# Head attention: the weights of two key chunks are added on GpSimd before TensorE sums them, and the ring of weights grows from two chunks to three

## The chip, the cores and the metric

The kernel runs on one core of a Trainium2 chip. A core has TensorE (PE, matrix products, with its own loads of weights, PEld), VectorE (DVE), ScalarE (ACT), GpSimd (POOL) and SyncE (SP, which here only issues transfers), and each works through its own list of instructions in order; between engines, semaphores say what may start. The metric is the device time of one execution in microseconds (us). Before the change it was 945.48 us, the median of three runs (945.34 to 948.28).

## The reference

Four layers follow each other on x of 8 x 256 x 512, each added to x: a latent cross-attention, a gated feed-forward layer, an eight-head attention against the context, and a layer of eight experts. The change touches the third only:

```python
def _L1_xattn_ref(q, k, v, gamma):        # q: layer norm of x; k = v = context
    qh = q.reshape(B, h, dq, Lq)           # h = 8 heads of 32 channels, Lq = Lk = 512
    qk = jnp.einsum('bhdq,bhdl->bhql', qh, kh) * scale
    sm = jax.nn.softmax(qk, axis=-1)
    ret = jnp.einsum('bhql,bhdl->bhdq', sm, vh)
    return gamma * ret.reshape(B, Dv, Lq)
```

A softmax needs, beside the weights exp(score - maximum), their sum over all 512 keys. That sum is what the change computes in another way.

## The kernel before

In `head_attention` (L721 and after) the channels lie on the partitions: a *unit* is one tile of 128 partitions, which is four heads (HU = 4) of 32 channels, and there are 16 units (NU). The 512 keys of a unit are four *chunks* of 128 (TC = 4). For each chunk c and each head h TensorE makes a tile of scores, 128 keys by 512 queries, in one of two PSUM buffers `B` (`scores`, L866), and ScalarE turns it into weights with an exponential into an SBUF tile `l_pt` (`weights`, L922). Then TensorE takes the four weight tiles of a chunk twice: as the moving operand of the product with the values (`product`, L877, into `PV`) and of a product with ones (`row_sums`, L885, into `SM`), which adds them over the keys. Both are f32 with a weight block of 32 columns, one for each head, so that the four heads lie side by side in the array. Both accumulate over the four chunks.

The weight tiles lie in a ring of RING = 2 chunks. ScalarE may overwrite a chunk when its row sums have been taken:

```python
wait(act, sum_ps, TC * u + c - RING + 1)
```

TensorE's order is written out by hand, as eight *cycles* (i = 0 to 7) a unit. Each has two score tiles, then in an even cycle a product and in an odd cycle the row sums of the same chunk, which lies one chunk back; odd cycles end with a quad of coarse scores (`a_quad`, L847) for a unit ahead, from which VectorE takes maxima (`maxima`, L983):

```python
scores(u, 2 * i)
scores(u, 2 * i + 1)
of, c = (u, i // 2 - 1) if i >= 2 else (u - 1, TC - 1)
if of >= 0:
    (row_sums if i % 2 else product)(of, c)
```

So in cycle 2 stands the product of chunk 0, in cycle 3 its row sums, in cycle 4 the product of chunk 1, in cycle 5 its row sums, and after these in cycle 5 the turn of the maxima (`rows`, L857). The quad in cycle 1 is that of (u + 1, 2), in cycle 3 of (u + 1, 3), in cycles 5 and 7 of (u + 2, 0) and (u + 2, 1).

VectorE's order in a unit: maxima (u + 1, 2), `statistics(u + 3)` (L988 to L992), maxima (u + 1, 3), `queries(u + 3)` (L997), maxima (u + 2, 0), `reciprocals(u - 1)` (L1001), maxima (u + 2, 1), `normalise(u - 1)` (L1007). ScalarE has beside the exponentials `result` after cycle 1 (L927), `totals` after 2 (L932), `logarithm` after 3 (L937) and `first_reciprocals` after 4 (L941), all of unit u - 1. GpSimd's order: `add(u - 2)` (L1076), `power(u + 3)` (L1050, waits for the statistics of VectorE), `keys(u + 3)` (L1057, L1059), `check_reciprocals(u - 1)` (L1072, waits for the reciprocals of ScalarE), `queries(u + 3)` (L1064, L1066). SyncE places the parts of keys and queries in `stack` (L809) a unit ahead.

Of the kernel before, what the change touches and what calls it, by code (L numbers as in the profile page):

```python
# [17 lines left out]
def wait(eng, sem, value):  # L18

    if isinstance(value, int) and value <= 0:  # L20
        return
    eng.wait_ge(sem, value)
# [700 lines left out]
def head_attention(nc, X, ident_f, ones_f, neg_half, ctx_in, ctxt_in, gamma_in, D, DH):  # L723
# [5 lines left out]
    CYCLES = STEPS // 2  # L729
    SCALE = float(DH) ** -0.5  # L730
    M0 = 3 * DH
    RING = 2
    st = ExitStack()
    with st:
        def sb(name, shape, dt=F32):
# [5 lines left out]
        def sem(name):  # L741
            return st.enter_context(nc.semaphore("l1_" + name))
# [24 lines left out]
        a_ps, max_ok, b_ps, b_ok = (sem(n) for n in ("aps", "max", "bps", "bok"))  # L767
        pv_ps, sum_ps, pv_ok, sums_ok = (sem(n) for n in ("pvps", "sumps", "pv", "sums"))
        ln_ok, r0_ok, sr_ok, ng_ok = (sem(n) for n in ("ln", "r0", "sr", "ng"))
        recip_ok, tx_ok, res_ok = (sem(n) for n in ("rec", "tx", "res"))  # L770

        block = st.enter_context(nc.Block())

# [15 lines left out]
        def weights_at(u, c, h):  # L789
            return PT[(TC * u + c) % RING][h]  # L790

# [45 lines left out]
        def _(pe):  # L837
# [40 lines left out]
                mm.then_inc(pv_ps, 1)  # L878

            def row_sums(u, c):  # L880
                if c == 0:
                    wait(pe, sums_ok, u)
                for h in range(HU):
                    cols = slice(DH * h, DH * h + DH)
                    mm = pe.matmul(SM[cols, :], ones_f[:, 0:DH], weights_at(u, c, h)[:, :], start=c == 0, stop=c == TC - 1)  # L885
                mm.then_inc(sum_ps, 1)

            for j in range(TC):
# [21 lines left out]
        @block.scalar  # L910
        def _(act):
            def rows_out(u):
                t = turn_of_rows(u)
                act.wait_ge(b_ps, t + 1)
                wait(act, row_in[u % 2], 16 * (u // 2))
                act.activation(mrow[u % 2][:, :], B[t % 2][0:HU * TC, 0:P], ACT.Copy).then_inc(b_ok, 1)

            def weights(u, s):
                c, h, t = s // HU, s % HU, turn_of_scores(u, s)
                act.wait_ge(b_ps, t + 1)  # L920
                wait(act, sum_ps, TC * u + c - RING + 1)
                act.activation(weights_at(u, c, h)[:, :], B[t % 2][:, :], ACT.Exp, scale=SCALE).then_inc(b_ok, 1)  # L922

            def result(u):
                act.wait_ge(pv_ps, TC * u + TC)
                wait(act, res_ok, u - 1)
                act.activation(pvs[u % 2][:, :], PV[:, :], ACT.Copy).then_inc(pv_ok, 1)  # L927

            def totals(u):
                act.wait_ge(sum_ps, TC * u + TC)  # L930
                wait(act, sr_ok, u)
                act.activation(sums[:, :], SM[:, :], ACT.Copy).then_inc(sums_ok, 1)  # L932

            def logarithm(u):
                act.wait_ge(sums_ok, u + 1)
                wait(act, recip_ok, u)
                act.activation(r0[:, :], sums[:, :], ACT.Ln).then_inc(ln_ok, 1)  # L937

            def first_reciprocals(u):
                act.wait_ge(ln_ok, u + 1)  # L940
                act.activation(r0[:, :], r0[:, :], ACT.Exp, scale=-1.0).then_inc(r0_ok, 1)  # L941

            def keys(u):
                act.wait_ge(kf_ok, 16 * u + 16)
                act.activation(kh[u % 2][:, :], kf[:, :], ACT.Copy).then_inc(kh_ok, 1)

            def queries(u):
                act.wait_ge(qf_ok, u + 1)
                act.activation(qh[u % 2][:, :], qf[:, :], ACT.Copy).then_inc(qh_ok, 1)

            act.preload_act_table_set("natural_log_exp_and_others")
            for u in range(2):
                keys(u)
                queries(u)
            rows_out(0)
            for u in range(NU):
                for i in range(CYCLES):
                    weights(u, 2 * i)
                    weights(u, 2 * i + 1)
                    if i == ROWS_AT // 2 - 1 and u + 1 < NU:  # L960
                        rows_out(u + 1)
                    if u:
                        if i == 1:
                            result(u - 1)
                        if i == 2:
                            totals(u - 1)
                        if i == 3:
                            logarithm(u - 1)
                        if i == 4:
                            first_reciprocals(u - 1)  # L970
            result(NU - 1)
            totals(NU - 1)
            logarithm(NU - 1)
            first_reciprocals(NU - 1)
# [71 lines left out]
        def _(pool):  # L1046
# [27 lines left out]
            def add(u):  # L1074
                pool.wait_ge(tx_ok, u + 1)
                pool.tensor_tensor(X[:, u, :], X[:, u, :], pvs[u % 2][:, :], ALU.add).then_inc(res_ok, 1)  # L1076

            for u in range(2):
                power(u)
                keys(u)  # L1080
                queries(u)
# [3 lines left out]
            for u in range(NU):  # L1085
                if u >= 2:
                    add(u - 2)
                if u + 3 < NU:
                    power(u + 3)
                    keys(u + 3)  # L1090
                if u:
                    check_reciprocals(u - 1)
                if u + 3 < NU:
                    queries(u + 3)
            add(NU - 2)
            check_reciprocals(NU - 1)
# [606 lines left out]
```

## Time and profile before

| | before |
|---|---|
| median of 3 runs | 945.48 us (945.34 to 948.28) |
| the profiled execution, its own time | 950.93 us |
| its span in the profile | 949.1 us |
| TensorE busy | 738.4 us (78%) |
| VectorE busy | 571.9 us (60%) |
| ScalarE busy | 400.9 us (42%) |
| GpSimd busy | 330.3 us (35%) |

The span is the stretch from the first to the last instruction of one profiled execution. Times of places are us from its start. "Busy" is the share in which an engine computes; the idle time that a row names is that just before its instructions, with what ended it. The profiled execution took some 5 us more than the median, so differences are worked out inside it and put on the median.

### The profile page before, as it was taken

How to read it: one execution, taken by the hardware profiler on the slowest of the kernel's cores; microseconds unless marked ns; L12 is line 12 of the kernel's file. 1: busy time of each engine (PE TensorE's matmuls, PEld its weight loads, DVE VectorE, ACT ScalarE, POOL GpSimd, SP SyncE). 2: the span in 40 equal slices, each digit the busy share in tenths (PEclk: the TensorE clock that was granted, in tenths of full speed). 3: DMA queues.
4: the chain of work that ended last, by engine and by line, in shares of the span. 5: the costliest groups of instructions: out<-in, count | busy, mean ns of one | idle time of the engine just before them, and what ended most of it. 6: DMA issues, size and time to landing. Idle time of an engine off the chain costs nothing. (4 is left out here: it accounts for less than half of the span.)

```text
span 949.1 us, 13635 instructions
## 1 busy us (share of the span) xinstructions
PE 738.4 (78%) x4259; PEld 308.5 (33%) x4288; DVE 571.9 (60%) x981; ACT 400.9 (42%) x727; POOL 330.3 (35%) x332
## 2 busy tenths in 40 slices
PE   3888888399999995699999999958002999999500
PEld 1344333144444442122222222135001555555300
DVE  5677775557668583889998898276300344344245
ACT  1534442164646462277877877845001222222100
POOL 2546454101120103235355443256471122122275
PEclk9999998779999998599999999979556999999955
DMA  7490100103030367343333332100355355655287
GB/s 265 77 122 24 44 1 0 62 0 108 15 122 2 121 250 271 83 105 98 96 96 96 96 101 73 30 1 1 119 205 145 100 124 134 134 129 130 79 261 256
DMA packets 98543, 99.12 MB, mean 104 GB/s; under 512 B 49448, under 2 KB 72872, under 8 KB 98224
## 3 DMA queue, kind: packets, MB, share of 16 engines
q1 hardware_dynamic: 90432, 78.25, 28.9%
q0 software_dynamic: 7328, 19.93, 8.7%
q8 instruction: 35, 0.57, 0.3%
q14 instruction: 28, 0.23, 0.1%
q10 hardware_dynamic: 720, 0.13, 0.1%
HBM read 51.82 MB, written 33.03 MB: 89 GB/s over the span
## 5 line engine op out<-in xcount | busy, mean ns | idle before, releaser
L983 DVE TENSOR_REDUCE l_negm<-l_a 128x2 f32<-128x1024 f32 x128 | 150.3, 1218 | 22.3 <-PE l_a L847 22.0
L922 ACT ACTIVATE l_pt<-l_b 128x512 f32<-128x512 f32 x256 | 138.9, 595 | 47.2 <-PE l_b L866 47.1
L1470 PE MATMUL ex_hp<-w1h,ex_xt 128*128 x312 | 78.6, 321 | 53.7 <-DMA ex_xt<-slots_x 53.4
L1556 POOL TENSOR_TENSOR ex_hl<-ex_hf,ex_hh 128x352 bf16<-128x352 f32 x39 | 33.2, 852 | 141.3 <-ACT ex_hh L1512 141.3
L866 PE MATMUL l_b<-l_stack 97*128 97x512 bf16 x256 | 79.4, 391 | 0.5 <-ACT l_pt L922 0.3
L568 PE MATMUL f_gp<-f_xt,wg 128*128 128x512 fp8e4 x256 | 67.4, 387 | 3.8 <-ACT f_y L611 2.7
L1490 PE MATMUL ex_yp<-w2h,ex_ht 128*128 (+1 forms) x215 | 68.8, 379 | 2.0 <-DVE ex_ht L1534 2.0
L877 PE MATMUL l_pv<-l_pt,l_vt 128*32 128x512 f32 x512 | 69.1, 612 | 0.0
L885 PE MATMUL l_sm<-l_pt,ones_f 128*32 128x512 f32 x512 | 68.3, 605 | 0.0
L1509 ACT ACTIVATE ex_hf<-ex_pre 128x352 f32<-128x352 f32 x39 | 19.3, 496 | 115.3 <-DVE ex_pre L1529 115.3
L568 PE MATMUL f_up_ps<-f_xt,wg 128*128 128x512 fp8e4 x256 | 67.0, 385 | 0.0
L1539 DVE COPY ex_y<-ex_yp 128x512 f32<-128x512 f32 x39 | 27.0, 691 | 53.3 <-PE ex_yp L1490 53.3
L717 POOL TENSOR_TENSOR X<-X,f_y 128x512 f32<-128x512 f32 x16 | 18.7, 1168 | 115.2 <-ACT f_y L611 115.2
L579 PE MATMUL f_yp<-wl,f_h 128*128 128x512 fp8e4 x256 | 55.9, 379 | 0.0
L1470 PEld LDWEIGHTS ex_hp<-w1h,ex_xt 128*128 128x128 bf16 x312 | 31.3, 100 | 69.3 <-issue 54.1
L670 DVE TENSOR_TENSOR f_prod<-f_gate,f_up 128x512 bf16<-128x512 bf16 x64 | 27.0, 422 | 43.9 <-ACT f_up L604 39.9
L1529 DVE TENSOR_TENSOR ex_pre<-ex_hp,ex_b1s 128x352 f32<-128x352 f32 x39 | 20.4, 524 | 54.0 <-PE ex_hp L1470 42.5
L1470 PE MATMUL ex_hp<-w1l,ex_xt 128*128 x156 | 50.2, 322 | 0.0
L602 ACT ACTIVATE f_gate<-f_gp 128x512 bf16<-128x512 f32 x64 | 38.2, 597 | 21.7 <-PE f_gp L568 21.7
L604 ACT ACTIVATE f_up<-f_up_ps 128x512 bf16<-128x512 f32 x64 | 38.2, 597 | 18.0 <-PE f_up_ps L568 18.0
L1490 PE MATMUL ex_yp<-w2l,ex_ht 128*128 (+1 forms) x117 | 44.3, 379 | 1.2 <-issue 0.2
L847 PE MATMUL l_a<-l_parts 32*128 32x512 bf16 x256 | 29.3, 408 | 17.5 <-DVE l_negm L983 10.5
(220 smaller groups left out, 1396.6 us busy)
## 6 DMA issues: line engine op xcount, KB each, us to landing
l_stack<-l_parts SPq DMA_DIRECT2D x192, 64.0 KB, 2.1
slots_x<-f_zeros SPq DMA_DIRECT2D x1, 9984.0 KB, 29.3
slots_y<-ex_y SPq DMA_DIRECT2D x39, 256.0 KB, 2.3
f_stage<-in_w SPq DMA_DIRECT2D x8, 704.0 KB, 4.0
l_ctx<-in_ctx SPq DMA_DIRECT2D x8, 512.0 KB, 5.3
f_stage<-in_w SPq DMA_DIRECT2D x8, 512.0 KB
l_kf<-in_ctx SPq DMA_DIRECT2D x16, 256.0 KB, 2.8
l_vt<-in_ctx_t SPq DMA_DIRECT2D x16, 256.0 KB, 3.0
```

What stands on the lines that cost most here:

```text
L568: mm = pe.matmul(bank[m % 2][:, :], wg8[:, c, col:col + P], xt8[:, c, :], start=c == 0, stop=c == FC - 1)
L579: mm = pe.matmul(YP[r % 2][:, :], h8[:, m, r * P:(r + 1) * P], wl8[:, m, :], start=m == 0, stop=m == HC - 1)
L602: act.activation(gate[m % 2][:, :], GP[m % 2][:, :], ACT.Gelu_apprx_tanh).then_inc(gate_ok, 1)
L604: act.activation(up[m % 2][:, :], UP[m % 2][:, :], ACT.Copy).then_inc(up_ok, 1)
L866: pe.matmul(B[t % 2][:, :], stack[u % 2][0:M0 + 1, 0, h, c * P:(c + 1) * P], stack[u % 2][0:M0 + 1, 1, h, :], start=True, stop=True).then_ ...
L877: mm = pe.matmul(PV[cols, :], VT[u % 2][:, c, cols], weights_at(u, c, h)[:, :], start=c == 0, stop=c == TC - 1)
L885: mm = pe.matmul(SM[cols, :], ones_f[:, 0:DH], weights_at(u, c, h)[:, :], start=c == 0, stop=c == TC - 1)
L922: act.activation(weights_at(u, c, h)[:, :], B[t % 2][:, :], ACT.Exp, scale=SCALE).then_inc(b_ok, 1)
L983: dve.tensor_reduce(negm[u % 2][:, 2 * half:2 * half + 2, j], A[half][:, :, :], AX.X, ALU.max, negate=True)\
L1470: mm = pe.matmul(HP[i % 2][:, 0:H], xt[i % AHEAD][:, xp * FC + f, :], w1p[wp][:, bass.ds(e, 1), f * H:(f + 1) * H], start=k == 0, stop=k = ...
L1490: mm = pe.matmul(YP[i % 2][:, :], ht[i % 2][0:K, n, m, :], w2p[wp][0:K, bass.ds(e, 1), m * D:(m + 1) * D], start=k == 0, stop=k == 3 * HC - 1)
L1556: pool.tensor_tensor(hl[i % 2][:, 0:H], hf[i % 2][:, :], hh[i % 2][:, 0:H], ALU.subtract).then_inc(hl_ok, 1)
```

## The change

GpSimd gets a new step, `pair_sums(u, h)`: for each of the four heads it adds the weights of chunk 1 to those of chunk 0, in the place of chunk 0, once the product of chunk 0 has read them and the weights of chunk 1 are there. TensorE leaves out the row sums of chunk 0 and takes those of the pair where those of chunk 1 stood, each head behind a wait of its own. The ring has three chunks, and the waits on `sum_ps` count three row sums a unit. In GpSimd's list three pair sums stand between `power` and `check_reciprocals`, the fourth behind it, and `keys(u + 3)` moves behind them.

```diff
-    RING = 2
+    RING = 3
+    SUMMED = (1, 1, 2, 3)
             def row_sums(u, c):
+
                 if c == 0:
+                    return
+                if c == 1:
                     wait(pe, sums_ok, u)
                 for h in range(HU):
                     cols = slice(DH * h, DH * h + DH)
-                    mm = pe.matmul(SM[cols, :], ones_f[:, 0:DH], weights_at(u, c, h)[:, :], start=c == 0, stop=c == TC - 1)
+                    if c == 1:
+                        pe.wait_ge(pair_ok, HU * u + h + 1)
+                    mm = pe.matmul(SM[cols, :], ones_f[:, 0:DH], weights_at(u, c if c > 1 else 0, h)[:, :], start=c == 1, stop=c == TC - 1)
                 mm.then_inc(sum_ps, 1)
@@ weights @@
-                wait(act, sum_ps, TC * u + c - RING + 1)
+                g = TC * u + c - RING
+                if g >= 0:
+                    act.wait_ge(sum_ps, (TC - 1) * (g // TC) + SUMMED[g % TC])
@@ totals @@
-                act.wait_ge(sum_ps, TC * u + TC)
+                act.wait_ge(sum_ps, (TC - 1) * (u + 1))
@@ gpsimd @@
+            def pair_sums(u, h):
+
+                pool.wait_ge(pv_ps, TC * u + 1)
+                pool.wait_ge(b_ok, done_scores(u, HU + h))
+                first, second = weights_at(u, 0, h), weights_at(u, 1, h)
+                pool.tensor_tensor(first[:, :], first[:, :], second[:, :], ALU.add).then_inc(pair_ok, 1)
+
@@ gpsimd, the loop over units @@
                 if u + 3 < NU:
                     power(u + 3)
-                    keys(u + 3)
+                for h in range(HU - 1):
+                    pair_sums(u, h)
                 if u:
                     check_reciprocals(u - 1)
+                pair_sums(u, HU - 1)
                 if u + 3 < NU:
+                    keys(u + 3)
                     queries(u + 3)
```

GpSimd's list of one unit before, from one `add` of `X` to the next `power`; l_rstd is written by `power`, l_parts by `keys` and `queries`, l_sr by `check_reciprocals`:

```order
L1076 TENSOR_TENSOR X<-X,l_pvs 128x512
L1050 TENSOR_TENSOR l_rstd<-l_veps,neg_half 128x1
L1057 CAST l_parts<-l_kf 128x512
L1059 TENSOR_TENSOR l_parts<-l_kf,l_parts 128x512
L1072 TENSOR_TENSOR l_sr<-l_sums,l_r 128x512
L1064 CAST l_parts<-l_qf 128x512
L1066 TENSOR_TENSOR l_parts<-l_qf,l_parts 128x512
```

And the same stretch now; L1091 is the new pair sum, and the other lines are some eight to ten further down in the file:

```order
L1084 TENSOR_TENSOR X<-X,l_pvs 128x512
L1058 TENSOR_TENSOR l_rstd<-l_veps,neg_half 128x1
L1091 TENSOR_TENSOR l_pt<-l_pt 128x512 x3
L1080 TENSOR_TENSOR l_sr<-l_sums,l_r 128x512
L1091 TENSOR_TENSOR l_pt<-l_pt 128x512
L1065 CAST l_parts<-l_kf 128x512
L1067 TENSOR_TENSOR l_parts<-l_kf,l_parts 128x512
L1072 CAST l_parts<-l_qf 128x512
L1074 TENSOR_TENSOR l_parts<-l_qf,l_parts 128x512
```

Three of the four pair sums stand behind `power` and ahead of `check_reciprocals`, the fourth behind both; the work on keys has moved behind all of them.

TensorE's list before, from the product of chunk 0 in cycle 2 to the turn of the maxima in cycle 5, with the semaphores that each waits for:

```order
L877 MATMUL l_pv<-l_pt,l_vt 32x512 x3
L866 MATMUL l_b<-l_stack 128x512 [waits l1_bok] x2
L885 MATMUL l_sm<-l_pt,ones_f 32x512 [waits l1_sums]
L885 MATMUL l_sm<-l_pt,ones_f 32x512 x3
L847 MATMUL l_a<-l_parts 128x512 [waits l1_max]
L847 MATMUL l_a<-l_parts 128x512
L847 MATMUL l_a<-l_parts 128x512 [waits l1_max]
L847 MATMUL l_a<-l_parts 128x512
L866 MATMUL l_b<-l_stack 128x512 [waits l1_bok] x2
L877 MATMUL l_pv<-l_pt,l_vt 32x512 [waits l1_bok]
L877 MATMUL l_pv<-l_pt,l_vt 32x512 x3
L866 MATMUL l_b<-l_stack 128x512 [waits l1_bok] x2
```

And now, from the scores of cycle 3 to the quad of cycle 5:

```order
L867 MATMUL l_b<-l_stack 128x512 [waits l1_bok] x2
L848 MATMUL l_a<-l_parts 128x512 [waits l1_max]
L848 MATMUL l_a<-l_parts 128x512
L848 MATMUL l_a<-l_parts 128x512 [waits l1_max]
L848 MATMUL l_a<-l_parts 128x512
L867 MATMUL l_b<-l_stack 128x512 [waits l1_bok] x2
L878 MATMUL l_pv<-l_pt,l_vt 32x512 [waits l1_bok]
L878 MATMUL l_pv<-l_pt,l_vt 32x512 x3
L867 MATMUL l_b<-l_stack 128x512 [waits l1_bok] x2
L891 MATMUL l_sm<-l_pt,ones_f 32x512 [waits l1_pair,l1_sums]
L891 MATMUL l_sm<-l_pt,ones_f 32x512 [waits l1_pair] x3
L858 MATMUL l_b<-ident_f,l_negm 16x128 [waits l1_bok,l1_max]
```

The row sums of cycle 3 are gone, and each of the four in cycle 5 waits for its own pair sum, `l1_pair`.

## Rows read from the trace of the kernel before

**Rows 1.** Busy time by stretch: units 1 to 12, units 13 and 14, unit 15.

```profile
409.12:574.80 165.68, 165.49 (x1180) 34.87 (x1177) 148.64 (x167) 130.21 (x252) 81.55 (x84) 1.00 0.38 97
574.80:601.91 27.11, 27.07 (x192) 5.58 (x189) 20.38 (x20) 21.70 (x42) 6.55 (x6) 1.00 0.32 79
601.91:616.30 14.39, 14.26 (x100) 2.71 (x96) 1.44 (x2) 11.17 (x22) 2.55 (x2) 1.00 0.01 1
```

The columns are the stretch, its length, then busy us and instructions of PE, PEld, DVE, ACT and POOL, the granted clock of TensorE, the share of the DMA engines, and GB/s.

**Rows 2.** Instructions in order of time, unit 12, TensorE: start, duration, instructions.

```profile
561.02 0.60 PE L866 MATMUL l_b<-l_stack 97*128 97x512 bf16 x2
561.56 1.07 PE L877 MATMUL l_pv<-l_pt,l_vt 128*32 128x512 f32 x8
...
563.09 1.06 PE L885 MATMUL l_sm<-l_pt,ones_f 128*32 128x512 f32 x8
564.09 0.40 PE L847 MATMUL l_a<-l_parts 32*128 32x512 bf16 x4
564.42 0.61 PE L866 MATMUL l_b<-l_stack 97*128 97x512 bf16 x2
564.96 1.07 PE L877 MATMUL l_pv<-l_pt,l_vt 128*32 128x512 f32 x8
...
569.88 1.06 PE L885 MATMUL l_sm<-l_pt,ones_f 128*32 128x512 f32 x8
570.77 0.38 PE L857 MATMUL l_b<-ident_f,l_negm 128*16 128x128 f32 x2
...
571.41 0.61 PE L866 MATMUL l_b<-l_stack 97*128 97x512 bf16 x2
...
574.80 0.60 PE L866 MATMUL l_b<-l_stack 97*128 97x512 bf16 x2
```

**Rows 3.** The same view and unit, the other engines.

```profile
564.52 2.36 DVE L983 TENSOR_REDUCE l_negm<-l_a 128x2 f32<-128x1024 f32 x2 [0.38 <-PE l_a L847]
...
566.79 0.68 DVE L988 BATCH_NORM_STATS2 l_st<-X 128x6 f32<-128x512 f32 x1
...
568.06 0.55 POOL L1050 TENSOR_TENSOR l_rstd<-l_veps,neg_half 128x1 f32<-128x1 f32 x1 [2.57 <-DVE l_veps L992]
...
569.21 0.63 ACT L941 ACTIVATE l_r<-l_r 128x512 f32<-128x512 f32 x1
```

**Rows 4.** Who waited for whom, from 395 to 617 us: total, times, longest.

```profile
POOL l_rstd L1050 <- DVE l_veps L992: 34.6, 13, 5.9
```

**Rows 5.** In order of time: two GpSimd sums of weight tiles in the first layer.

```profile
28.47 1.27 POOL L436 TENSOR_TENSOR l_psa<-l_pt 128x512 f32<-128x512 f32 x1 [5.61 <-ACT l_pt L289]
29.69 1.26 POOL L437 TENSOR_TENSOR l_psb<-l_pt 128x512 f32<-128x512 f32 x1
```

**Rows 6.** In order of time: VectorE and GpSimd at once, in two units.

```profile
422.69 1.07 DVE L1001 SCALAR_TENSOR_TENSOR l_sr<-l_sr,l_r 128x512 f32<-128x512 f32 x1 [0.67 <-POOL l_sr L1072]
423.30 1.49 POOL L1066 TENSOR_TENSOR l_parts<-l_qf,l_parts 128x512 bf16<-128x512 f32 x1
...
435.65 1.16 POOL L1066 TENSOR_TENSOR l_parts<-l_qf,l_parts 128x512 bf16<-128x512 f32 x1
```

**Rows 7.** In order of time: unit 0, GpSimd's power and TensorE's row sums of chunk 1.

```profile
400.52 0.55 POOL L1050 TENSOR_TENSOR l_rstd<-l_veps,neg_half 128x1 f32<-128x1 f32 x1 [2.13 <-DVE l_veps L992]
...
404.20 1.07 PE L885 MATMUL l_sm<-l_pt,ones_f 128*32 128x512 f32 x8
```

**Rows 8.** In order of time: TensorE in the first layer, two rounds of its loop.

```profile
47.91 0.38 PE L191 MATMUL l_sm<-l_dev,mean_f 128*128 128x1 f32 x2 [1.76 <-DVE l_dev L363]
48.15 5.38 PE L197 MATMUL l_pv<-l_pt,l_gx 128*128 128x512 f32 x8
...
68.17 0.38 PE L191 MATMUL l_sm<-l_dev,mean_f 128*128 128x1 f32 x2 [1.17 <-DVE l_dev L363]
68.42 3.68 PE L197 MATMUL l_pv<-l_pt,l_gx 128*128 128x512 f32 x8
```

**Rows 9.** Busy time by stretch, columns as in rows 1: inside the first of these rounds.

```profile
50.00:52.00 2.00, 2.00 (x3) 0.66 (x2) 0.72 (x3) 0.00 (x0) 1.53 (x2) 0.50 1.00 109
```

More of the change, by code:

```diff
@@ L769, in head_attention @@
         ln_ok, r0_ok, sr_ok, ng_ok = (sem(n) for n in ("ln", "r0", "sr", "ng"))
-        recip_ok, tx_ok, res_ok = (sem(n) for n in ("rec", "tx", "res"))
+        recip_ok, tx_ok, res_ok, pair_ok = (sem(n) for n in ("rec", "tx", "res", "pair"))
         block = st.enter_context(nc.Block())
```

## The prediction

> **What bounds the kernel now.** I read the busy time by stretch first, for the attention alone, since only it is changed. The reader is to see that TensorE has no idle time there: 165.49 us busy of 165.68 in units 1 to 12, which is 165.68 / 12 = 13.81 us a unit, at the full granted clock, with GpSimd busy for 81.55 us, 6.8 us a unit [rows 1]. So TensorE is the bound, GpSimd is half empty, and four f32 matmuls a unit less look like a gain. Whether they are one is told by the instructions in order of time, for one unit, since each engine works in order: what has to be seen is when, in a unit, GpSimd can begin, and when TensorE will want its result.
>
> All places below are counted from the first scores of a unit, 561.02 us for unit 12 [rows 2]. TensorE's times: quad (u + 1, 2) at +3.07, scores of cycle 2 at +3.40, product of chunk 0 at +3.94 for 1.07, so done at +5.0; row sums of chunk 1 at +8.86, the turn of the maxima at +9.75, the scores of cycle 6 at +10.39, and the next unit at +13.78 (574.80) [rows 2]. A pair of scores with a product is 561.56 - 561.02 = 0.54 and 1.00 more, about 1.53 us a cycle, and the quad another 0.33 (564.42 - 564.09) [rows 2].
>
> **What is saved.** The row sums of chunk 0 occupy TensorE for as long as those of any chunk do: from 563.09 to the quad at 564.09, 1.00 us [rows 2]. 16 units make 16.0 us, if what comes after in the unit can move up by as much. Nothing else of TensorE's goes.
>
> **What is added, and where it stands.** GpSimd gets 64 sums of 128 x 512 f32. The same form on weight tiles is in the first layer, 1.27 us each, and back to back they start 29.69 - 28.47 = 1.22 us apart [rows 5]. That is 4.9 us a unit: 6.8 + 4.9 = 11.7 of 13.8, so GpSimd's busy time would still fit. Its order does not.
>
> 1. The pair sums stand behind `power(u + 3)` in GpSimd's list. `power` waits for statistics which VectorE makes after the maxima of quad (u + 1, 2): the quad is at +3.07, VectorE starts on it at +3.50 (564.52) after an idle 0.38, the statistics start at +5.77 (566.79), and GpSimd's power runs from +7.04 (568.06) for 0.55 to +7.59 [rows 3]. That this is a real wait and no accident of one unit: GpSimd waited 34.6 us for it in 13 units [rows 4]. Nothing of the change moves it, as everything ahead of it in the unit stays where it was. So the first pair sum starts at about +7.56, 2.5 us after its operands are there.
> 2. Behind it: three pair sums, `check_reciprocals`, the fourth pair sum. The reciprocals that the check wants end at 569.21 + 0.63, +8.8 [rows 3], before the check's turn at 7.56 + 3 x 1.22 = +11.2, so nothing more is waited for. The fourth pair sum starts at 7.56 + 4 x 1.22 = +12.44 and ends 1.27 later, at +13.7. With 0.1 us for the semaphore (an estimate: VectorE starts at 564.52 on a quad that ends at 564.09 + 0.40 [rows 2, 3], 0.03 us, and I round up) TensorE's fourth row sum starts at +13.8.
> 3. TensorE wants it at +8.86 before, and, with the row sums of chunk 0 gone, about 1 us earlier. It stands at the head of TensorE's list in cycle 5, and behind it wait the turn of the maxima, the quad (u + 2, 0), and all scores of cycles 6 and 7; ScalarE has nothing to do without these. The heads before come at +8.9, +10.2 and +11.4, and are hidden.
> 4. One head alone needs two f32 passes one after another, as the four heads side by side do, so I take the same 0.89 us from its start to the turn of the maxima (569.88 to 570.77) and 1.53 to the scores of cycle 6 (571.41); from there the unit ends 3.39 later (574.80) as before [rows 2]. The new unit is 13.8 + 1.53 + 3.39 = 18.7 us, 4.9 more than 13.81. The 1.00 us saved lies inside the stall and buys nothing.
> 5. VectorE's `queries` now falls among the pair sums (it comes after maxima that end at about +9.4). Where the two engines met in the trace, GpSimd's 1.16 us became 1.49, 0.33 more, the first being that of 435.65, the second that of 423.30, behind VectorE's instruction of 422.69 [rows 6]. I add 0.3: 5.2 us a unit. From below this cost is 0 (VectorE may lose the race each time). The Trainium skill (SBUF — State Buffer, "Who interferes with whom") says that the pair of ports is an exclusive lock, held for the whole instruction by whoever starts first. By that rule the loser waits up to the 1.07 us which VectorE's instruction is shown with [rows 6], part of which was its own wait; charged in full it would be 12 x 0.7 = 9 us on the kernel above my sum, but the row shows 0.33, and I go by it.
>
> Units 1 to 12: 12 x 5.2 = 62.4 us.
>
> Unit 0 has no check, and its power runs from 400.52 to 401.07 [rows 7]. Four pair sums end at 401.04 + 3 x 1.22 + 1.27 = 405.97, with semaphore 406.1, where the row sums of chunk 1 started at 404.20 [rows 7]: 1.9 later, with the meeting of point 5 2.2 us.
>
> Units 13 to 15 have no power, so that the pair sums start when the product of chunk 0 is done, +5.1. Three of them end at +8.8, just as the reciprocals do [rows 3]; check and fourth sum follow to 8.8 + 1.22 + 1.27 = +11.3, TensorE starts at +11.4 where it was +8.86: 2.5 us each. Unit 14 and 15 have fewer quads, which shortens both sides alike to within 0.3 us: unit 15 was 8 x 1.53 = 12.3 and becomes 11.0 + 1.0 + 3.06 = 15.1. Together 7.7 us.
>
> The moved `keys(u + 3)` and `queries(u + 3)` (3.6 us of GpSimd) start at +13.7 and end at +17.4 of a unit of 19; what needs them is a unit ahead, and the next power is at +7.04 of the next unit, so the length of the unit hides them. SyncE's load of keys stands behind them at about +15.6; its next transfer, the stack of the next unit, waits for that unit's start at +19 anyway. VectorE's sequence from the quad of cycle 5 to its next maxima keeps its length, relative to the scores of cycle 6, so it still arrives in time. The third chunk of the ring gives ScalarE nothing: its exponentials follow scores, and TensorE's list sets these.
>
> **The sum.** 2.2 + 62.4 + 7.7 = 72.3 us on the profiled execution of 950.93, to 1023; on the median of 945.48, from which that execution is 5 us away for reasons that have no part in this, 1017.8. The forecast is 1018 us. Its own range is 1005 to 1032: 0.3 us a unit less for point 5 (4 us), 0.5 a unit either way for the gaps and the length of a lone head (8 us), 6 us more for the lock.
>
> **The rivals.**
>
> *TensorE's clock falls in the stall.* In the first layer TensorE was idle for 1.76 us before a short matmul [rows 8], and a little later its granted clock was 0.50, which is 1.2 GHz, while it was busy without a gap [rows 9]; the eight matmuls then took 5.38 us where they take 3.68 in another round [rows 8]: 1.7 us for one fall. In the new kernel TensorE has from about +8 to +13.8 only three lone heads of some 0.9 us, and before the fourth an idle 1.5 us, in every unit. For it speaks this likeness; against it, that the other round had 1.17 us idle at the same place and its eight matmuls ran at full pace [rows 8]. At 1.7 us in 15 units it adds 26 us, to 1044; if every unit pays the passes of the lone head and both last cycles in full at 1.2 GHz, 0.9 + 3.4 = 4.3 us, it is up to 64 more. Chance 0.26.
>
> *Power is no bar.* If VectorE's statistics came much earlier, the pair sums would start at +5.1 in all units, and the last at +10.1, as in units 13 to 15. The cost would be 15 x 2.5 + 2.2 = 40 us: 986. For it speaks that VectorE has idle time in a longer unit; against it, that the quad which it waits for is fixed at +3.07, and that GpSimd waited for power in 13 units [rows 4]. Chance 0.06.
>
> *The sums are hidden: faster.* If the fourth pair sum ended before TensorE comes to it at about +7.9, the row sums saved would all count: 16 x 1.0 = 16 us, 930. It turns at one place, the end of the fourth pair sum in cycle 5; from the product's end at +5.0 there are 2.9 us for 4.9 us of sums, even without power and check. For it speaks only GpSimd's idle half [rows 1]. Chance 0.02.
>
> *Something else by which the time stays near.* No mechanism that I can find; 0.01 within 0.3%, 0.01 a little slower.
>
> **How the numbers follow.** The forecast has 0.64. The range that is to hold the time 8 times in 10 takes its own range and the nearer half of the clock's case: 1003 to 1054. Faster by over 0.3% 0.02, within 0.3% 0.01, slower 0.97; 0.3% is about what a measurement of this kernel can tell from no change.
>
> **What would show it.** In the profile after: TensorE's idle time before the new row sums, put down to GpSimd's pair sums, about 1.5 us before the fourth head and 5 us less its own work in all per unit; units of 19 us; GpSimd's three pair sums, check and fourth sum back to back behind power; a TensorE busy share near 67% in the attention. The first step would be wrong if the pair sums start at +5 in units 1 to 12; the fourth, if the lone head takes half of 0.89; the clock's rival is right if the granted clock in units 1 to 12 is below 1.00. The forecast as a whole is wrong if units stay under 16 us.

## The result, and the profile after

The changed kernel takes 1016.5 us, the median of four runs (1014.9 to 1020.6), against 946.9 us for the kernel before with four runs (945.3 to 949.7): 69.6 us more, a ratio of 1.072 with a 95% interval of 1.069 to 1.075. The forecast was 1018 us, from 72.3 us more.

The page of the profile shows where the time is by who waited. These are four of its groups, with busy time in us and mean ns of one between the bars, and behind it the idle time of the engine just before them and what ended it:

```profile
PE 771.1 (76%) x4160; PEld 312.2 (31%) x4160; DVE 576.2 (57%) x981; ACT 398.6 (39%) x727; POOL 405.9 (40%) x396
...
L991 DVE TENSOR_REDUCE l_negm<-l_a 128x2 f32<-128x1024 f32 x128 | 150.4, 1220 | 83.9 <-PE l_a L848 83.9
L930 ACT ACTIVATE l_pt<-l_b 128x512 f32<-128x512 f32 x256 | 139.2, 599 | 45.5 <-PE l_b L867 45.5
L891 PE MATMUL l_sm<-l_pt,ones_f 128*32 128x512 f32 x384 | 95.9, 605 | 33.7 <-POOL l_pt L1091 32.4
...
L1091 POOL TENSOR_TENSOR l_pt<-l_pt 128x512 f32<-128x512 f32 x64 | 82.0, 1303 | 7.7 <-PE l_pv L878 7.7
```

The row sums have fallen from 512 matmuls to 384, and TensorE now stands idle before them until GpSimd's pair sums are there, which was nowhere so before. VectorE, which waited 22.0 us for the quads on the page before, waits 83.9: it is held by the same stall. The 32.4 us are only part of the stall, since TensorE's matmuls of the heads before count as busy in it.

In order of time, TensorE in unit 11, which begins at 594.69; columns as in [rows 2]:

```profile
594.69 0.60 PE L867 MATMUL l_b<-l_stack 97*128 97x512 bf16 x2
...
597.76 0.40 PE L848 MATMUL l_a<-l_parts 32*128 32x512 bf16 x4
598.09 0.60 PE L867 MATMUL l_b<-l_stack 97*128 97x512 bf16 x2
598.62 1.07 PE L878 MATMUL l_pv<-l_pt,l_vt 128*32 128x512 f32 x8
...
600.16 0.83 PE L848 MATMUL l_a<-l_parts 32*128 32x512 bf16 x4
...
602.50 0.60 PE L867 MATMUL l_b<-l_stack 97*128 97x512 bf16 x2
603.65 2.18 PE L891 MATMUL l_sm<-l_pt,ones_f 128*32 128x512 f32 x4 [0.55 <-POOL l_pt L1091]
606.19 1.04 PE L891 MATMUL l_sm<-l_pt,ones_f 128*32 128x512 f32 x2 [0.36 <-POOL l_pt L1091]
608.63 0.62 PE L891 MATMUL l_sm<-l_pt,ones_f 128*32 128x512 f32 x1 [1.40 <-POOL l_pt L1091]
608.74 0.38 PE L858 MATMUL l_b<-ident_f,l_negm 128*16 128x128 f32 x2
609.08 0.59 PE L891 MATMUL l_sm<-l_pt,ones_f 128*32 128x512 f32 x1
...
609.93 0.60 PE L867 MATMUL l_b<-l_stack 97*128 97x512 bf16 x2
...
613.33 0.60 PE L867 MATMUL l_b<-l_stack 97*128 97x512 bf16 x2
```

And GpSimd in the same unit:

```profile
601.73 0.55 POOL L1058 TENSOR_TENSOR l_rstd<-l_veps,neg_half 128x1 f32<-128x1 f32 x1 [2.56 <-DVE l_veps L1000]
...
602.24 3.89 POOL L1091 TENSOR_TENSOR l_pt<-l_pt 128x512 f32<-128x512 f32 x3
...
606.10 1.26 POOL L1080 TENSOR_TENSOR l_sr<-l_sums,l_r 128x512 f32<-128x512 f32 x1
...
607.32 1.26 POOL L1091 TENSOR_TENSOR l_pt<-l_pt 128x512 f32<-128x512 f32 x1
```

Up to the scores of cycle 3 the unit is that of before: the quad at +3.07, the product at +3.93. Power starts at +7.04, the pair sums at +7.55, the check follows without a gap, and the fourth pair sum ends at 608.58, +13.89. The fourth head starts 0.05 us later, and the unit ends at 613.33, 18.64 after its start, where before it was 13.78 [rows 2]. The product of chunk 0 had been done since 599.69: 2.5 us passed before GpSimd, held at power, began.

### The profile page after: what moved, and what is told of

Read it like the earlier page. It is cut to its first block and busy times, and to the rows that moved or that the text cites. A ratio compares the mean times of both kernels' runs of the same rounds, so it can differ in the third digit from the quotient of the medians.

```text
span 1013.1 us, 13547 instructions
## 1 busy us (share of the span) xinstructions
PE 771.1 (76%) x4160; PEld 312.2 (31%) x4160; DVE 576.2 (57%) x981; ACT 398.6 (39%) x727; POOL 405.9 (40%) x396
## 5 line engine op out<-in xcount | busy, mean ns | idle before, releaser
L991 DVE TENSOR_REDUCE l_negm<-l_a 128x2 f32<-128x1024 f32 x128 | 150.4, 1220 | 83.9 <-PE l_a L848 83.9
L891 PE MATMUL l_sm<-l_pt,ones_f 128*32 128x512 f32 x384 | 95.9, 605 | 33.7 <-POOL l_pt L1091 32.4
L1091 POOL TENSOR_TENSOR l_pt<-l_pt 128x512 f32<-128x512 f32 x64 | 82.0, 1303 | 7.7 <-PE l_pv L878 7.7
L1508 PE MATMUL ex_yp<-w2h,ex_ht 128*128 (+1 forms) x234 | 76.0, 379 | 2.0 <-DVE ex_ht L1552 2.0
L848 PE MATMUL l_a<-l_parts 32*128 32x512 bf16 x256 | 34.7, 412 | 18.3 <-DVE l_negm L991 10.5
L1084 POOL TENSOR_TENSOR X<-X,l_pvs 128x512 f32<-128x512 f32 x16 | 20.3, 1271 | 66.6 <-DVE l_pvs L1015 66.6
```

The lines of the kernel that those rows point to most:

```text
L848: mm = pe.matmul(A[h // 2][:, h % 2, :], qh[u % 2][of_head, j * P:(j + 1) * P], kh[u % 2][of_head, :], start=True, stop=True)
L991: dve.tensor_reduce(negm[u % 2][:, 2 * half:2 * half + 2, j], A[half][:, :, :], AX.X, ALU.max, negate=True)\
L1091: pool.tensor_tensor(first[:, :], first[:, :], second[:, :], ALU.add).then_inc(pair_ok, 1)
L1508: mm = pe.matmul(YP[i % 2][:, :], ht[i % 2][0:K, n, m, :], w2p[wp][0:K, bass.ds(e, 1), m * D:(m + 1) * D], start=k == 0, stop=k == 3 * HC - 1)
```

## The experiments

The first four take the changed kernel apart. All ratios are to the kernel before in the same batch of runs, with 95% intervals; "per unit" is from the profile, the mean distance of the first twelve additions to X, 13.80 us before and 18.78 after.

**Check behind the pair sums.** One of the three steps ahead of the last pair sum goes behind it.

```diff
-                for h in range(HU - 1):
+                for h in range(HU):
                     pair_sums(u, h)
                 if u:
                     check_reciprocals(u - 1)
-                pair_sums(u, HU - 1)
```

> The changed kernel with one step moved in GpSimd's list: check_reciprocals stands behind all four pair sums, no longer ahead of the fourth. Theory (the chain: power, pair sums, then TensorE's last head, sets the length of a unit): the fourth pair sum ends one step of 1.22 us earlier in units 1 to 15, a unit is 18.64 - 1.22 = 17.4 us, and the time 1016.5 - 15 x 1.22 = 998 us. Rival (what costs is GpSimd's load as such, through the ports that it shares with VectorE or through memory): the load is the same, so the time stays at 1016 us within 3.

Measured: 997.5 us, ratio 1.0505 (1.0475 to 1.0534), 17.43 us per unit, 1.21 less than the 18.64 of the changed kernel. That is 19.0 us less than the changed kernel for a move of one instruction of 1.26 us in 15 units. The load is the same; the rival is out.

**Power behind them too**, shown against the changed kernel:

```diff
-                if u + 3 < NU:
-                    power(u + 3)
-                for h in range(HU - 1):
+                for h in range(HU):
                     pair_sums(u, h)
+                if u + 3 < NU:
+                    power(u + 3)
                 if u:
                     check_reciprocals(u - 1)
-                pair_sums(u, HU - 1)
```

> The changed kernel with GpSimd's order turned so that all four pair sums come first, then power, then check_reciprocals, keys and queries. Theory (the chain): the pair sums start when the product of chunk 0 is done, at +5.1, as they do in units 13 to 15 of the changed kernel; the fourth ends at 5.1 + 3 x 1.22 + 1.27 = +10.0, TensorE's scores of cycle 6 start 1.4 later and the unit ends at +14.8: 1.0 over the kernel before in 15 units, 946.9 + 15 = 962 us, between 957 and 968. VectorE's queries, which wait for power, come 3 us later, which I take to be hidden by TensorE's stall. Rival (load): 1016 us. Second rival (power late is itself the bar, because VectorE, held at queries, makes TensorE wait for maxima): over 975 us.

Measured: 962.5 us, ratio 1.0141 (1.0114 to 1.0169), 14.84 us per unit. In order of time, GpSimd and TensorE around the row sums of one unit, which begins at 524.7:

```profile
529.85 4.96 POOL L1091 TENSOR_TENSOR l_pt<-l_pt 128x512 f32<-128x512 f32 x4 [0.64 <-PE l_pv L878]
534.76 0.55 POOL L1058 TENSOR_TENSOR l_rstd<-l_veps,neg_half 128x1 f32<-128x1 f32 x1
```

```profile
533.09 1.60 PE L891 MATMUL l_sm<-l_pt,ones_f 128*32 128x512 f32 x6
534.86 0.62 PE L891 MATMUL l_sm<-l_pt,ones_f 128*32 128x512 f32 x1 [0.17 <-POOL l_pt L1091]
534.97 0.38 PE L858 MATMUL l_b<-ident_f,l_negm 128*16 128x128 f32 x2
```

The pair sums begin with the end of the product, and TensorE is idle for only 0.17 us before the last head. So 54.0 of the 69.6 us were GpSimd's order: power ahead of the sums and the check among them. Late power did not matter. What is left, 1.04 us per unit, is still the chain: the heads come one by one as the sums are ready, and from the first head to the turn of the maxima it is 534.97 - 533.09 = 1.88 us, where four heads together take 0.89 [rows 2].

**No pair sum at all**, that is the row sum less by itself, with GpSimd's order of before. This version leaves the weights of chunk 0 out of the row sums, so it does not compute the softmax; it only gives a time.

```diff
-                    if c == 1:
-                        pe.wait_ge(pair_ok, HU * u + h + 1)
-                    mm = pe.matmul(..., weights_at(u, c if c > 1 else 0, h)[:, :], start=c == 1, ...)
+                    mm = pe.matmul(..., weights_at(u, c, h)[:, :], start=c == 1, ...)
...
-                    pair_sums(u, h)
```

> The changed kernel without any pair sum: the weights of chunk 0 are left out of the row sums, TensorE sums chunks 1 to 3 without waiting for GpSimd, and GpSimd's order is that of before. It says what a row sum less is worth by itself. If TensorE alone sets the pace it is 16 x 1.00 = 16 us, 931 us. My theory is less: in the changed kernel's trace the scores of cycle 5 come at +7.81 against +8.33 before, since ScalarE with its extra work in cycles 2 to 4 does not let TensorE go faster; so 16 x 0.5 = 8 us, 939 us, between 935 and 943.

Measured: 942.6 us, ratio 0.9939 (0.991 to 0.9968), 13.47 us per unit. The number is within what I gave, and far from 16 us: a third of the row sum's 1.00 us comes out, 0.33 us per unit. The reason I gave for it, ScalarE, fell later.

**The load without the wait.** GpSimd adds two tiles of its own where the pair sums stood, in the changed kernel's order. TensorE's row sums are those of the version without pair sums, which wait for nothing and leave chunk 0 out.

```diff
-                first, second = weights_at(u, 0, h), weights_at(u, 1, h)
-                pool.tensor_tensor(first[:, :], first[:, :], second[:, :], ALU.add).then_inc(pair_ok, 1)
+                wait(pool, pair_ok, HU * u + h + 2)
+                pool.tensor_tensor(apart[0][:, :], apart[0][:, :], apart[1][:, :], ALU.add).then_inc(pair_ok, 1)
```

> The changed kernel with GpSimd's 64 sums of the same form and at the same places in its list, but on two tiles of zeros of its own; TensorE sums chunks 1 to 3 and waits for no pair (the weights of chunk 0 are left out of the row sums). The load stays, the wait goes. Theory (the chain): the wait is the whole loss, so the time falls to that of the kernel without pair sums, 939 us, plus at most 0.3 us a unit from the ports shared with VectorE: 937 to 946 us. Rival (load): it stays above 1000 us.

Measured: 954.1 us, ratio 1.0050 (1.0031 to 1.0069), 14.25 us per unit. The rival is out, for the wait was most of the loss. But the time is outside the 937 to 946 us that I gave: the sums in this place cost 11.5 us over the run without them, where I had allowed 5. Groups of VectorE's instructions, first in the run without sums:

```profile
L1007 DVE SCALAR_TENSOR_TENSOR l_sr<-l_sr,l_r 128x512 f32<-128x512 f32 x16 | 14.7, 920 | 22.8 <-POOL l_sr L1078 22.8
...
L1003 DVE TENSOR_SCALAR l_qf<-X,l_mv,l_rstd 128x512 f32<-128x512 f32 x14 | 9.4, 672 | 0.0
```

and in this one:

```profile
L1008 DVE SCALAR_TENSOR_TENSOR l_sr<-l_sr,l_r 128x512 f32<-128x512 f32 x16 | 25.7, 1607 | 18.9 <-POOL l_sr L1079 18.9
...
L1004 DVE TENSOR_SCALAR l_qf<-X,l_mv,l_rstd 128x512 f32<-128x512 f32 x14 | 18.4, 1313 | 0.0
```

The same two instructions of VectorE take 0.69 and 0.64 us more each, 1.3 us a unit, for they stand in time beside GpSimd's sums. VectorE is then busy for 96.1 of 100 us (440 to 540 us), columns as in [rows 1]:

```profile
440.00:540.00 100.00, 93.50 (x634) 20.52 (x630) 96.09 (x99) 74.68 (x147) 86.28 (x78) 1.00 0.35 93
```

That looks as if VectorE set the pace, but the idle time of TensorE is elsewhere. Its group of the scores on the page of the run without sums, and on the page of this run:

```profile
L867 PE MATMUL l_b<-l_stack 97*128 97x512 bf16 x256 | 80.1, 392 | 1.0 <-ACT l_pt L928 0.7
```

```profile
L868 PE MATMUL l_b<-l_stack 97*128 97x512 bf16 x256 | 80.0, 391 | 9.6 <-issue 8.7
```

It stands idle before the first scores of a unit, for which the profile names no engine. In the kernel these wait for two things that SyncE places, the stack and, behind it in SyncE's list, the row of maxima (`l_mrow`). In order of time, from the unit that begins at 521.75:

```profile
522.98 1.16 POOL L1066 TENSOR_TENSOR l_parts<-l_kf,l_parts 128x512 bf16<-128x512 f32 x1
...
524.17 0.34 SPq L800 DMA_DIRECT2D l_kf<-in_ctx  x1
524.62 7.65 SPq L811 DMA_DIRECT2D l_stack<-l_parts  x12
...
531.04 0.39 PE L859 MATMUL l_b<-ident_f,l_negm 128*16 128x128 f32 x2
...
532.95 0.56 SPq L820 DMA_DIRECT2D l_stack<-l_mrow  x1
...
534.76 0.40 PE L849 MATMUL l_a<-l_parts 32*128 32x512 bf16 x4
...
535.71 0.59 PE L868 MATMUL l_b<-l_stack 97*128 97x512 bf16 x2 [0.55 <-issue]
```

GpSimd's keys, behind the sums and the check, end at 524.14. Only then does SyncE load the next keys, and only behind that load does it place the stack, 2.87 us after the unit began, where in the run without sums it does so as the unit begins (484.11 against 484.37). So the row of maxima goes out 1.91 us after TensorE's turn, where in that run it is 0.72; it lands about 2.5 us later (median of this transfer in the DMA view, 500 to 512 us). The next unit's scores start 4.67 us after the turn, where they take 4.05 there. Over the eleven units with turns from 430.84 to 573.58 the mean is 4.87, 0.82 us late each, 9 us in all. So most of the 11.5 us is a second wait for GpSimd, through SyncE; it is read from the trace, and no run moves the keys or that load by itself. How much VectorE's longer instructions cost beside it is not separated.

**The ring alone.**

```diff
-    RING = 2
+    RING = 3
```

> The kernel before with a ring of three chunks and nothing else. Theory: ScalarE's exponentials follow the scores, and TensorE's written order sets these, so a third chunk gives and costs nothing: within 0.3% of the kernel before. Rival (two chunks hold ScalarE back, so that part of the change is a gain that the wait hides): 0.5% or more faster.

Measured: 950.7 us, ratio 0.9994 (0.9976 to 1.0011). No effect can be seen.

The next ask whether the idea can pay at all, and why a row sum less brings so little.

**The pair taken later.** A ring of four; TensorE sums chunk 2 and then the pair, both in cycle 7. GpSimd's order is two pair sums, power, two more, then the check, keys and queries (its lines are not shown).

```diff
-    RING = 3
-    SUMMED = (1, 1, 2, 3)
+    RING = 4
+    SUMMED = (2, 2, 1, 3)
             def row_sums(u, c):
-                if c == 0:
+                if c < 2:
                     return
...
+                if c == 2:
+                    for h in range(HU):
+                        cols = slice(DH * h, DH * h + DH)
+                        pe.wait_ge(pair_ok, HU * u + h + 1)
+                        mm = pe.matmul(SM[cols, :], ones_f[:, 0:DH], weights_at(u, 0, h)[:, :], start=False, stop=False)
+                    mm.then_inc(sum_ps, 1)
```

> A version that keeps the pair sums and takes them off the path: a ring of four chunks; TensorE sums chunk 2 first in cycle 7 and the pair right behind it in the same cycle, some 5 us later than in the changed kernel; GpSimd takes two pair sums, power, two more, then check_reciprocals, keys and queries, so that the fourth is ready at about +10.6, before TensorE comes to it at +12.8. Theory: TensorE no longer waits, and what is left is what the run without the wait showed, VectorE held by GpSimd at the shared ports, 0.6 to 0.7 us a unit over the kernel without pair sums: about 952 us, 947 to 957. Rival (with the wait gone the row sums saved count): 942 us or less. Rival (a wait stays somewhere): over 960 us.

Measured: 953.8 us, ratio 1.0037 (1.0014 to 1.0059), 14.18 us per unit. The size is as expected, and there is no wait for a pair sum. But the cause in the trace is not the one that I had named. In order of time, one unit that begins at 507.4:

```profile
514.29 2.35 DVE L994 TENSOR_REDUCE l_negm<-l_a 128x2 f32<-128x1024 f32 x2
...
516.69 0.39 PE L858 MATMUL l_b<-ident_f,l_negm 128*16 128x128 f32 x2 [0.85 <-DVE l_negm L994]
...
519.42 1.06 PE L888 MATMUL l_sm<-l_pt,ones_f 128*32 128x512 f32 x8
...
520.30 1.04 PE L894 MATMUL l_sm<-l_pt,ones_f 128*32 128x512 f32 x8
```

TensorE comes to the turn of the maxima in cycle 5 with nothing left to sum ahead of it, and waits 0.85 us for VectorE's maxima of quad (u + 1, 3), which end at 514.29 + 2.35 = 516.64, +9.2. These stand behind the maxima of (u + 1, 2) and the statistics. After that turn come two sets of row sums. The maxima are no later than in the run without sums, where they end at +9.2 as well; it is TensorE that comes earlier. So the unit is a chain through VectorE in its first half and TensorE's fuller list in its second.

**ScalarE's steps moved.** As "no pair sum at all", with:

```diff
-                        if i == 3:
+                        if i == 5:
                             logarithm(u - 1)
-                        if i == 4:
+                        if i == 6:
                             first_reciprocals(u - 1)
```

> The kernel without pair sums (the weights of chunk 0 are left out of the row sums) with two of ScalarE's steps moved: logarithm from cycle 3 to 5, first_reciprocals from 4 to 6, out of the cycles that have become short. It asks why one row sum less brought 5 us and not 16. If ScalarE's extra steps in cycles 2 to 4 are the bound: TensorE's cycle 3 falls from 1.30 to 0.87 us, 16 x 0.4 = 6 us less than the 942.5 us of the kernel with these steps in place, 936 us. Rival (VectorE, busy for some 12.4 us a unit and waiting for the ports, is): it stays at 941 to 944 us, and TensorE waits for maxima instead.

Measured: 947.8 us, ratio 0.9976 (0.9955 to 0.9996), 13.81 us per unit. It did not fall to the 936 us of my theory, and in this run the little gain is nearly gone, which neither side had said. In order of time, one place of it:

```profile
517.93 1.27 POOL L1078 TENSOR_TENSOR l_sr<-l_sums,l_r 128x512 f32<-128x512 f32 x1 [1.41 <-issue]
...
519.23 1.07 DVE L1007 SCALAR_TENSOR_TENSOR l_sr<-l_sr,l_r 128x512 f32<-128x512 f32 x1 [0.94 <-POOL l_sr L1078]
...
520.22 2.34 DVE L989 TENSOR_REDUCE l_negm<-l_a 128x2 f32<-128x1024 f32 x2
...
522.22 0.80 PE L848 MATMUL l_a<-l_parts 32*128 32x512 bf16 x4
```

The later reciprocals make the check on GpSimd late, VectorE waits 0.94 us for it, takes 1.07 us for a step of 0.68, and starts on the maxima behind it that much later. TensorE's quad of cycle 1 waits for these with its second half: it takes 0.73 us to the scores behind it, where 0.33 is the usual, in each of nine units. So ScalarE's steps where they stood were not the bound, and moved they make a new wait.

**The maxima first.** As "no pair sum at all", with VectorE's statistics out of that chain, and keys behind the check on GpSimd:

```diff
                 if u + 1 < NU:
                     maxima(u + 1, 2)
-                if u + 3 < NU:
-                    statistics(u + 3)
-                if u + 1 < NU:
                     maxima(u + 1, 3)
                 if u + 3 < NU:
-                    queries(u + 3)
+                    statistics(u + 3)
                 if u + 2 < NU:
                     maxima(u + 2, 0)
+                if u + 3 < NU:
+                    queries(u + 3)
```

> The kernel without pair sums (the weights of chunk 0 are left out of the row sums), with VectorE's order turned: the maxima of quad (u + 1, 3) right behind those of (u + 1, 2), then the statistics, the maxima of (u + 2, 0), and queries; GpSimd takes power, check_reciprocals, keys, queries. It asks again why a row sum less brought 5 us and not 16. Theory (the turn of the maxima in cycle 5 waits for VectorE: quad at +3.07, maxima, statistics, maxima end at +9.3, and it ends the unit 4.0 later, 13.3 to 13.4): with the statistics out of that chain its end falls to +8.2 and the unit to the 12.9 us of TensorE, 0.4 less in some 14 units: 6 us below the run without pair sums, 0.988 of the kernel before. Rival (VectorE's whole load, 12.4 us a unit and the port waits, is the bound whatever its order): 0.994 of the kernel before, as that run.

Measured: 940.4 us, ratio 0.9900 (0.9866 to 0.9934), 13.27 us per unit. It is the best of the runs that leave the sum out, though its interval overlaps that of the run with the old order, and of the 0.4 us a unit that I gave for it 0.20 is there. The wait in question, and one that I had overlooked, in the run with the old order:

```profile
476.52 0.83 PE L848 MATMUL l_a<-l_parts 32*128 32x512 bf16 x4
...
476.96 0.09 PEld L848 LDWEIGHTS l_a<-l_parts 32*128 32x128 bf16 x2 [0.35 <-DVE l_negm L989]
...
477.92 2.35 DVE L989 TENSOR_REDUCE l_negm<-l_a 128x2 f32<-128x1024 f32 x2
...
480.33 0.39 PE L858 MATMUL l_b<-ident_f,l_negm 128*16 128x128 f32 x2
```

The maxima end at 477.92 + 2.35 = 480.27, and TensorE's turn starts 0.06 later, but that holds it for only 0.05 us: the turn comes 0.93 us behind the start of the row sums, in the new order 0.88. More of the 0.20 is the quad of cycle 1, which in three of fourteen units of the old order took 0.51 to 0.70 us to the next scores for a wait of the same kind, and in the new 0.32 or 0.33 in all units from 413 to 559 us.

The wait that stays is at the quad of cycle 3 (476.52). With the row sums ahead of it gone, its second half comes before VectorE has finished the maxima of the quad before. From its start to the next scores it is 0.76 us or more in every unit of both runs from 400 to 580 us, where it was 0.33 [rows 2], and these scores take 0.05 more. So of the 1.00 us taken out, 0.43 and 0.05 come back at once, and 13.78 - 1.00 + 0.48 = 13.26 is the 13.27 us of this run. The changed kernel has the same quad, 0.83 long at 600.16. It is read from the traces; no run moves that quad.

**The same order with the pair sums**, in the version with the pair in cycle 7 and GpSimd's four sums, power, check, keys, queries; the edits are the last two together.

> The version with the pair taken in cycle 7 and a ring of four, with the same turn of VectorE's order, and GpSimd's order four pair sums, power, check_reciprocals, keys, queries. Its full result is computed. In the version before it TensorE waited 0.85 us a unit at the turn of the maxima for VectorE, in cycle 5. Theory: with that wait gone the unit falls from 14.18 to 13.2 to 13.4 us, limited then by VectorE and its port waits; against the kernel before 0.45 us a unit less, about 0.992 to 0.996. Rival (the port waits of VectorE among back-to-back GpSimd sums cost as much as the order gains): 1.00 to 1.005.

Measured: 952.4 us, ratio 1.0022 (0.9997 to 1.0047), 13.97 us per unit. The time is the rival's, but the trace does not show its cause, the ports. The maxima no longer hold the turn in cycle 5; with no row sums ahead of it TensorE now waits there for ScalarE's exponentials, and the quad of cycle 3 is split as before:

```profile
525.80 0.83 PE L848 MATMUL l_a<-l_parts 32*128 32x512 bf16 x4
...
529.42 0.38 PE L858 MATMUL l_b<-ident_f,l_negm 128*16 128x128 f32 x2 [0.67 <-ACT l_pt L933]
```

The scores of cycle 5 take 1.27 us to the turn in place of 0.54, and with the 0.48 us at the quad that is the whole unit: 13.78 - 1.00 + 0.73 + 0.48 = 13.99, measured 13.97.

**And with the kernel before**, all row sums in place.

> The kernel before, all its row sums in place and no pair sums, with VectorE's and GpSimd's order of the run that had the maxima first. Theory: with four row sums a unit TensorE is busy for all of the 13.8 us, so that the order of VectorE brings nothing by itself: within 0.3% of the kernel before. Rival (the gain of that run came from the order, and not from the row sum left out with it): 0.995 or less.

Measured: 953.3 us, ratio 1.0037 (1.0018 to 1.0056), 14.15 us per unit: a little slower, just outside the 0.3% that I gave (which its interval still holds) and on the other side from the rival. So the order is no gain of its own. VectorE's queries meet GpSimd's keys there, and TensorE's quad of the next unit's cycle 1 is split by the wait for the maxima behind them. It lasts 0.77 us in place of 0.40, and this 0.37 is what the unit has grown by, 14.15 against 13.78:

```profile
534.42 1.47 DVE L997 TENSOR_SCALAR l_qf<-X,l_mv,l_rstd 128x512 f32<-128x512 f32 x1
534.45 1.16 POOL L1058 TENSOR_TENSOR l_parts<-l_kf,l_parts 128x512 bf16<-128x512 f32 x1
...
538.44 0.77 PE L847 MATMUL l_a<-l_parts 32*128 32x512 bf16 x4
```

No version with the pair sums was faster than the kernel before.

## Why the prediction was right, point by point

*The chain.* It is the one predicted, and its places are off by 0.2 us at most: power at +7.04, the sums from +7.55, the fourth done at +13.89 where I had +13.7 and 0.3 for the ports. Moving single steps of it off the path moved the time by what they had held up (997.5 and 962.5 us, forecast 998 and 962), so it is shown and not only read. One place was off by more: TensorE comes to the row sums of cycle 5 not 1 us earlier than before but 0.5, since its scores of cycle 5 are at +7.81 where they were at +8.33; the quad of cycle 3 keeps the rest. The stall hid that. Of the signs that I gave, the idle time before the fourth head came (1.40 us, forecast 1.5), and the busy share of 67% did not: in units 1 to 12 TensorE counts as busy for 195.6 of 225.2 us, 87%, because a head alone lasts 1.04 us (606.19), as long as four side by side [rows 2], and four of them come one after another.

*The sum by stretches.* Unit 0 was 15.11 us (394.01 to 409.12) and is 16.96 (389.77 to 406.73): 1.9 more, forecast 2.2. Units 1 to 12 were 165.7 and are 631.97 - 406.73 = 225.2: 59.6 more, forecast 62.4. From unit 13 to the start of the last row sums it was 615.12 - 574.80 = 40.3 and is 679.63 - 631.97 = 47.7: 7.3 more, forecast 7.7. Together 68.8, against 69.6 between the medians. The two profiled executions as a whole are only 64.0 us apart (1013.1 and 949.1 us of span): the one before was slower ahead of the attention, which it began 4.2 us later (394.01 against 389.77). So the stretches fit the forecast better than the two whole executions would show.

*The ports.* Forecast 0.3 us a unit. Four steps of 1.22 would be 4.88; from the first pair sum to the fourth it is 607.32 - 602.24 = 5.08, so 0.20. As the row in the trace before said, VectorE takes little from GpSimd; the whole of VectorE's instruction was not lost to the chain. The run without the wait shows the other side, which the prediction had no need of because the stall hid it: VectorE's two instructions take 1.3 us a unit more. What that costs in time is not shown.

*The lone head.* This term was mis-sized. I took 1.53 us from its start to the scores of cycle 6, as for four heads; it is 609.93 - 608.63 = 1.30, since the turn of the maxima starts 0.11 us behind the head (608.74) and ahead of its second pass (609.08), where behind four heads it came after 0.89 [rows 2]. By the prediction's own sign (half of 0.89) this step was wrong in its picture; it cost only 0.23 us a unit, and that is why the number held. This is most of the 0.36 by which the 18.64 us unit is below the 19.0 forecast.

*The clock.* The rival with 0.26 happened once in 16 units. By stretch of 4 us, columns as in [rows 1]:

```profile
532.00:536.00 4.00, 3.46 (x14) 0.64 (x18) 1.11 (x1) 0.92 (x3) 3.84 (x5) 0.60 0.01 1
```

The granted clock is at 1.2 GHz for most of it, after a stall like that of all other units, and the distance of the additions to X there is 541.97 - 521.79 = 20.18 us against 18.64 in the units around. One fall cost 1.5 us; the row of the first layer had said 1.7 [rows 8]. Why this stall and not the others is open.

*The saving.* I counted it as nothing, since it lies inside the stall. That held for the time; the size of 1.00 us a unit that I gave for it outside of the stall did not. With nothing to wait for it is 0.33, or 0.53 with another order of VectorE. So the rival that put the kernel at 930 us had the wrong size as well: even with free sums it would have been about 940 in the orders tried. The prediction's picture of TensorE as the only bound, from its full busy time [rows 1], was too simple. The quad of cycle 3 was just behind VectorE's maxima, and as soon as TensorE's list got shorter ahead of it, it waited there. That the first guess, ScalarE, was wrong is shown by a run; that it is this quad, and in the run with ScalarE's steps moved the quad of cycle 1 too, is read from their traces and not tested by itself.

That 1018 came within 1.5 us of 1016.5 is partly luck. The lone head and the ports together were 0.36 us a unit below the forecast, 4 us over the units; the one fall of the clock, 1.5 us, which the forecast did not have, went the other way; and the median of the kernel before is 1.4 us above the one that the 72.3 us were added to.

## What to carry to other kernels

Before an engine with idle time is given work that another engine waits for, look at where in its list the work stands, and what it must wait for there: here half of GpSimd's time was free, and 54 of the 70 us lost were two steps standing ahead of the new one. Look as well at what stands behind it: in the run where nobody waited for the sums, keys that came later held a transfer, and the transfer held TensorE. Then ask where the result is wanted, and count from the operands to there; with 2.9 us for 4.9 us of sums no order would do. And test what the removed work is worth by leaving it out, before building what replaces it: that run would have said 5 us of 16, and no version that kept the sums got even that back.

## What the runs showed of the hardware that was not expected

The turn of the maxima (16 columns of weights) starts while the two-pass f32 matmul ahead of it, a lone head in other columns, is still in its first pass: at 608.74 against 608.63, 0.11 us behind.

VectorE's two-input and scaling instructions on f32 in SBUF, 0.68 and 0.54 us at their shortest, took 1.61 and 1.31 us on average beside GpSimd's sums in the run without the wait, while these sums stayed at 1.27 (they were 1.30 in the changed kernel). It is not always VectorE that is longer: GpSimd's cast of the keys took 1.08 us in that run at 521.82, and its cast of the queries 0.61 at 524.09. The Trainium skill (SBUF — State Buffer, "Who interferes with whom") says that the engine which starts first holds the pair of ports for the whole instruction and that issue order decides who blocks. At 520.69 VectorE's instruction takes 1.74 us; it started 0.07 behind a sum of 1.26 (520.62), and the 1.19 left of that sum and its own 0.68 make 1.87, so this place agrees within 0.13 us.
